# Second layer of a two-layer transformer on one core: the first attention on its latent, the last batch's gating on two engines, weights loaded earlier

## The reference

```python
# third block: 8 heads of 64, latent of 64
q = (x @ Wq.T).reshape(b, t, 8, 64)
kv_latent = x @ Wkv_down.T
k = (kv_latent @ Wk_up.T).reshape(b, t, 8, 64)
v = (kv_latent @ Wv_up.T).reshape(b, t, 8, 64)
scores = einsum('bqhd,bkhd->bhqk', q, k) * 64 ** -0.5
out = einsum('bhqk,bkhd->bqhd', softmax(scores), v).reshape(b, t, 512) @ Wo.T
# fourth block
wv = topk_mask(x @ Ws, 2) * sigmoid(x @ Ws)              # b t h e
v = einsum('bthe,btek->bhtk', wv, einsum('btd,edk->btek', x, Wv))
attn = softmax attention of (x @ Wq) and (x @ Wk) over v
out = einsum('bthe,bthk,ekd->btd', topk_mask(x @ Wd, 2), attn, Wo)
```

## Time and profile before

| | |
|---|---|
| three timed runs | 3288.48, 3310.31, 3311.98 us, median 3310.31 |
| the profiled execution | 3291.7 us, its span 3289.6 us |
| busy over the span | PE 2514.8 us (76%), DVE 2017.9 (61%), POOL 1914.4 (58%), ACT 1706.0 (52%) |
| second layer | from 1784.5 us to the end |
| mean granted clock of TensorE | 0.845 of full speed (2.4 GHz; 0.5 is the lower level, 1.2 GHz) |

### The profile page before, as it was taken

The page is one execution under the profiler, slowest core; times in us unless marked ns, Lnnn a source line. Parts: engine busy times, 40 slices in busy tenths (PEclk is TensorE's granted clock), DMA queues, the critical chain, the costliest instruction groups (busy, mean ns, idle before and its releaser), DMA issues. The chain is left out here.

```text
span 3289.6 us, 31482 instructions
## 1 busy us (share of the span) xinstructions
PE 2514.8 (76%) x10185; PEld 1158.7 (35%) x10185; DVE 2017.9 (61%) x3044; ACT 1706.0 (52%) x2409; POOL 1914.4 (58%) x1911
## 2 busy tenths in 40 slices
PE   4567676766766676752994889899999999999984
PEld 2222222322322232221552344444444444444432
DVE  4798878687868787731332366565647464656541
ACT  1677776776776777850221345444444444444440
POOL 0555566666665675864775106565748383746495
PEclk7678787877777777775997899999999999999996
DMA  2000000000101000011997100000000000000000
GB/s 90 14 0 7 9 14 15 13 14 15 14 15 14 15 7 7 15 21 38 268 267 197 20 1 1 1 14 7 14 7 1 20 1 20 1 7 1 7 1 13
DMA packets 94883, 99.04 MB, mean 30 GB/s; under 512 B 19552, under 2 KB 91488, under 8 KB 94688
## 3 DMA queue, kind: packets, MB, share of 16 engines
q1 hardware_dynamic: 69984, 73.53, 7.9%
q0 software_dynamic: 24704, 23.22, 3.9%
HBM read 74.24 MB, written 26.80 MB: 31 GB/s over the span
## 5 line engine op out<-in xcount | busy, mean ns | idle before, releaser
L848 POOL TENSOR_TENSOR TT<-TT,SS 128x512 f32<-128x512 f32 x512 | 652.1, 1308 | 401.8 <-ACT SS L779 401.5
L1467 ACT ACTIVATE PR<-S,NM 128x512 f32<-128x512 f32 x512 | 347.5, 683 | 589.3 <-DVE NM L1588 589.3
L1588 DVE TENSOR_REDUCE NM<-S 128x2 f32<-128x1024 f32 x256 | 313.1, 1223 | 254.0 <-PE S L1382 252.4
L371 PE MATMUL OB<-TT,VAL 128*17 128x512 f32 x1024 | 349.4, 786 | 86.9 <-ACT TT L787 86.9
L612 DVE TENSOR_SCALAR TT<-SC 128x1024 f32<-128x1024 f32 x256 | 311.4, 1216 | 121.4 <-POOL TT L848 60.7
L1382 PE MATMUL S<-KT,QT 64*128 64x512 f32 x1024 | 328.4, 661 | 0.0
L614 DVE SCALAR_TENSOR_TENSOR SS<-SC,TT 128x1024 f32<-128x1024 f32 x256 | 313.5, 1225 | 20.2 <-issue 1.3
L853 POOL DMA_INDIRECT slot_tokens<-TID,IDX x256 | 258.9, 1011 | 111.7 <-issue 84.7
L1411 PE MATMUL OT<-PT,VN 128*64 128x512 f32 x1024 | 283.5, 633 | 3.1 <-ACT PT L1473 2.3
L1393 PE MATMUL TP<-ident,PR 128*128 128x128 f32 x2048 | 274.6, 277 | 3.9 <-DVE PT L1593 3.0
L1393 PEld LDWEIGHTS TP<-ident,PR 128*128 128x128 f32 x2048 | 226.6, 141 | 143.3 <-issue 117.5
(11 more groups left out here) (227 smaller groups left out, 4281.7 us busy)
## 6 DMA issues: line engine op xcount, KB each, us to landing
WG<-w_gu SPq DMA_DIRECT2D x64, 384.0 KB
WD<-w_dn SPq DMA_DIRECT2D x64, 128.0 KB
stream<-rows SPq DMA_DIRECT2D x1, 4224.0 KB, 16.5
XL<-x SPq DMA_DIRECT2D x8, 512.0 KB, 4.2
X<-x SPq DMA_DIRECT2D x8, 512.0 KB, 3.9
rows<-XL SPq DMA_DIRECT2D x8, 512.0 KB, 8.9
slot_tokens<-TID,IDX POOLq DMA_INDIRECT x256
stream<-X SPq DMA_DIRECT2D x8, 512.0 KB, 3.6
```

What stands on the lines that cost most here:

```text
L371: ins = pe.matmul(OB[r:r + DH0 + 1, :], values_of[:, mt, h, :], TT[:, h % RING, mt, :], start=(mt == 0), stop=(mt == NT - 1))
L848: ins = pool.tensor_tensor(tt[:, mt, :], tt[:, mt, :], ss[:, mt, :], ALU.add)
L1467: act.activation(PR[s % 2][h2][:], S[s % 2][:, h2, :], ACT.Exp, bias=NM[:, s % 2, h2:h2 + 1], accum_out=SM[:, pair % 2, j, h2:h2 + 1]).the ...
L1588: dve.tensor_reduce(NM[:, s % 2, :], S[s % 2][:], AX, ALU.max, negate=True).then_inc(sems["peak"], 1)
```

## The change

**First attention in the latent space.** With q = x Wq and k = c Wk (c the latent), q k' = (x Wq Wk') c'. So Wq and Wk of a head are multiplied once into a combined weight `q1a` (width 64 a head, as before), the keys of all heads are the latent, and no `keys1` is left. In the same way the values are the latent (`values1` is now one item of four transposes of it), and Wv goes into the output weight `o1a`. `down1` is loaded twice side by side, so that the latent lies on both halves of the partitions. The combining is new: `absorb` ahead of run 0 (16 transposes into banks of S, 16 small products, five ACT copies) and two items `absorb_out` in run 0. Three `queries1` of batch 0 and its `values1` move from `FIRST` into run 0.

**Start.** SP loads both streams of batch 0, DVE adds them and does the normalisation itself. The weights Wq, Wkv_down, Wk_up, Wv_up are loaded in `stage_two`, after expert 3's.

**Last batch's gating.** POOL gates the odd heads into a buffer of its own (`gate_last`, h = 2 * pair + 1), DVE the even ones into another, `join` adds the two. The last batch's `turn_out2` and `product_out2` use the seven other PSUM banks instead of `BK`.

```diff
@@ stage_two, SP @@
                 sp.dma_start(WD[u][P - FC:P, 1, :], w_dn[e][P:F, :]).then_inc(sems[f"weights_in{u}"], 16)
+                if e == UN - 1:
+                    for dst, src in early:
+                        sp.dma_start(dst, src).then_inc(sems["weights_now"], 16)
@@ tables @@
 PREP_1 = table(
-    (0, 4, 1, "turn_norm", 0), (0, 5, 1, "turn_norm", 1), (0, 5, 2, "latent", 0),
-    (0, 6, 1, "queries1", 0), (0, 6, 2, "keys1", 0), (0, 7, 2, "queries1", 1), (0, 8, 1, "keys1", 1),
-    (0, 9, 1, "queries1", 2), (0, 9, 2, "keys1", 2), (0, 10, 1, "queries1", 3), (0, 10, 2, "keys1", 3),
-    (0, 11, 2, "values1", 0), (0, 12, 1, "values1", 1), (0, 13, 1, "values1", 2), (0, 14, 1, "values1", 3))
+    (0, 4, 1, "turn_norm", 0), (0, 5, 1, "turn_norm", 1), (0, 6, 1, "latent", 0), (0, 8, 1, "queries1", 0),
+    (0, 9, 1, "values1", 0), (0, 10, 1, "queries1", 1), (0, 12, 1, "queries1", 2), (0, 13, 1, "queries1", 3))
+PREP_FIRST = table((0, 0, 1, "queries1", 1), (0, 1, 1, "values1", 0), (0, 2, 1, "queries1", 2), (0, 3, 1, "queries1", 3),
+                   (0, 8, 2, "absorb_out", 0), (0, 11, 1, "absorb_out", 1))
-OUT_2_TAIL = table((0, 4, 3, "turn_out2", 0), ...
+OUT_2_TAIL = table((0, 4, 3, "join", 0), (0, 4, 3, "turn_out2", 0), ...
-    FIRST = table((0, 0, 3, "merge", 0), (0, 0, 3, "stats", 0), ..., (0, 0, 3, "latent", 0),
-                  *[(0, 0, 3, part, i) for i in range(C1) for part in ("queries1", "keys1")],
-                  *[(0, 0, 3, "values1", j) for j in range(NT)])
+    FIRST = table((0, 0, 3, "absorb", 0), (0, 0, 3, "stats_first", 0), ...,
+                  (0, 0, 3, "latent", 0), (0, 0, 3, "queries1", 0))
@@ stage_three, SP @@
-            for b in range(2):
-                sp.dma_start(X[b][:], x_b[b]).then_inc(sems[f"x_in{b}"], 16)
-            for dst, src in loads_now:
-                sp.dma_start(dst, src).then_inc(sems["weights_now"], 16)
-            for b in range(2, XN_RING):
+            sp.dma_start(X[0][:], x_b[0]).then_inc(sems["x_in0"], 16)
+            sp.dma_start(XN[:], x2_b[0]).then_inc(sems["x_in0"], 16)
+            for b in range(1, XN_RING):
@@ TensorE @@
+            def values1(v, i, b):
+                bank = item(v, "free_d")
+                need(v, "latent", b, 0)
+                for j in range(NT):
+                    ins = pe.transpose(bank[:, j * R1:(j + 1) * R1], KT[set_for(1, b)][0:R1, 0, j * P:(j + 1) * P],
+                                       ident[0:R1, 0:R1])
+            def absorb(v, i, b):
+                pe.wait_ge(sems["weights_now"], 16 * NOW)
+                ...
+                pe.wait_ge(sems["wide_in"], 3)
+                for c in range(DC):
+                    for pair in range(PAIRS1):
+                        for h2 in range(2):
+                            lo, at = DH1 * h2, (PAIRS1 * c + pair) * R1
+                            ins = pe.matmul(TP[h2][:, at:at + R1], q1t[lo:lo + DH1, pair, c * P:(c + 1) * P],
+                                            kvt[lo:lo + DH1, 0, pair, :], start=True, stop=True)
+            def absorb_out(v, i, b):
+                bank = item(v, "free_a")
+                for a in range(2):
+                    for h2 in range(2):
+                        lo, pair = DH1 * h2, 2 * i + a
+                        ins = pe.matmul(bank[lo:lo + R1, a * D:(a + 1) * D], kvt[lo:lo + DH1, 1, pair, :],
+                                        o1[lo:lo + DH1, pair, :], start=True, stop=True)
@@ scores, attend @@
-                                    KT[r % 2][lo:lo + DH1, pair, :], start=True, stop=True)
+                                    KT[r % 2][lo:lo + DH1, 0 if kind == 1 else pair, :], start=True, stop=True)
-                    h, lo = 2 * pair + h2, DH1 * h2
+                    h, lo = 2 * pair + h2 if kind == 2 else 0, DH1 * h2
@@ DVE @@
+            def stats_first(v, i, b):
+                dve.wait_ge(sems["x_in0"], 32)
+                dve.tensor_tensor(flat, flat, XN[:].rearrange("p j d -> p (j d)"), ALU.add)
+                dve.drain()
+                measure(X[0])
+                dve.wait_ge(sems["rstd1"], 1)
+                for j in range(NT):
+                    ins = dve.tensor_scalar(XN[:, j, :], X[0][:, j, :], mv[:, j, 0:1], rstd[:, j:j + 1],
+                                            ALU.subtract, ALU.mult)
+            def gate(v, pair, b):
+                if b < B - 1:
+                    return
+                h = 2 * pair
+                dve.drain()
+                for j in range(NT):
+                    ins = dve.tensor_tensor((gt if pair else gl)[:, j], ..., ALU.mult)
+                if pair:
+                    dve.drain()
+                    ins = dve.tensor_tensor(GL_DVE, GL_DVE, GT_DVE, ALU.add)
+            def join(v, i, b):
+                dve.wait_ge(sems["gadd"], H1 * B)
+                dve.drain()
+                dve.tensor_tensor(GL_POOL, GL_POOL, GL_DVE, ALU.add).then_inc(sems["joined"], 1)
```

More of the change, by code:

```diff
@@ L1108, in timetable @@
             put(r, OUT_2, b - 1)
+    put(0, PREP_FIRST, 0)
     for b in range(1, XN_RING):
@@ L1186, in stage_three @@
     READER = dict(
-        turn_norm="dd", latent="a", queries1="aaaa", keys1="dada", values1="adad", product_out1="dddd", gates="d",
+        turn_norm="dd", latent="a", queries1="aaaa", values1="d", absorb_out="aa", product_out1="dddd", gates="d",
         experts="aaaa", queries2="aaaa", keys2="aaaa", turn_out2="ddd", product_out2="dddd",
     )
-    FIRST = table((0, 0, 3, "merge", 0), (0, 0, 3, "stats", 0), *[(0, 0, 3, "turn_norm", c) for c in range(DC)], (0, 0, 3, "latent", 0),
-                  *[(0, 0, 3, part, i) for i in range(C1) for part in ("queries1", "keys1")],
-                  *[(0, 0, 3, "values1", j) for j in range(NT)])
+    FIRST = table((0, 0, 3, "absorb", 0), (0, 0, 3, "stats_first", 0), *[(0, 0, 3, "turn_norm", c) for c in range(DC)],
+                  (0, 0, 3, "latent", 0), (0, 0, 3, "queries1", 0))
     def reader(part, i):
@@ L1331, in turn_out2 @@
             def turn_out2(v, c, b):
-                bank = item(v, "free_d")
-                if c == 0:
+                last = b == B - 1
+                bank = free_bank(c) if last else item(v, "free_d")
+                if last and c == 0:
+                    pe.wait_ge(sems["joined"], 1)
+                elif c == 0:
                     pe.wait_ge(sems["gadd"], v.next("gadd", H1))
@@ L1336, in turn_out2 @@
                 for j in range(NT):
-                    ins = pe.transpose(bank[:, j * P:(j + 1) * P], GO[:, j, lo:lo + P], ident[:])
+                    ins = pe.transpose(bank[:, j * P:(j + 1) * P], (GL_POOL if last else GO)[:, j, lo:lo + P], ident[:])
                 ins.then_inc(sems["item_d"], 1)
             def product_out2(v, j, b):
-                bank = item(v, "free_d")
+                bank = free_bank(3 + j) if b == B - 1 else item(v, "free_d")
+                if b == B - 1 and v.all_due("free_d"):
+                    pe.wait_ge(sems["free_d"], v.value + 3)
                 for c in range(3):
@@ L1378, in scores @@
                     need(v, f"queries{kind}", b, pair)
-                    need(v, f"keys{kind}", b, pair)
+                    need(v, *(("latent", b, 0) if kind == 1 else ("keys2", b, pair)))
+                if (r, s) == (0, 0):
+                    pe.wait_ge(sems["wide_in"], 5)
                 for h2 in range(2):
@@ L1406, in attend @@
                         pe.wait_ge(sems["vh"], v.next("vh", 2))
[L1407 to L1408 removed]
+                if kind == 1 and pair == 0 and m == 0:
+                    need(v, "values1", b, 0)
                 for h2 in range(2):
[L1410 removed]
+                    h, lo = 2 * pair + h2 if kind == 2 else 0, DH1 * h2
                     ins = pe.matmul(OT[lo:lo + DH1, :], VN[r % 2][:, m, h * DH1:(h + 1) * DH1], PT[pair % 2][h2][:, m, :],
@@ L1544, in product_out2 @@
                 dve.wait_ge(sems["item_d"], v.next("item_d"))
-                dve.tensor_tensor(x[:, j, :], x[:, j, :], BK[:, 0:D], ALU.add).then_inc(sems["free_d"], 1)
+                bank = free_bank(3 + j) if b == B - 1 else BK
+                dve.tensor_tensor(x[:, j, :], x[:, j, :], bank[:, 0:D], ALU.add).then_inc(sems["free_d"], 1)
                 if j == NT - 1:
@@ L1673, in mix_values, with gate_last @@
                     ins.then_inc(sems["vh"], 1)
+            def gate_last(v, pair, b):
+                pool.wait_ge(sems["head"], v.next("head"))
+                pool.drain()
+                gl = GL_POOL.rearrange("p j (e d) -> p j e d", e=SE)
+                gt = GT[:].rearrange("p j (e d) -> p j e d", e=SE)
+                h = 2 * pair + 1
+                for j in range(NT):
+                    ins = pool.tensor_tensor((gt if pair else gl)[:, j], AH[pair % 2][:, j, 1, :].unsqueeze(1).to_broadcast([P, SE, DH1]),
+                                             MO[b % 2][:, j, h, :].unsqueeze(2).to_broadcast([P, SE, DH1]), ALU.mult)
+                if pair:
+                    pool.drain()
```

(5 more changed lines are left out.)

124 lines of the change are left out of this document (89 added, 35 removed).

## The result

| | before | after |
|---|---|---|
| timed, median (lowest to highest) | 3309.01 us (3288.48 to 3311.98) | 3197.28 us (3192.03 to 3206.46) |
| profiled execution, span | 3291.7, 3289.6 us | 3206.46, 3204.7 us |
| second layer begins | 1784.5 us | 1800.9 us |
| second layer, to the end | 1505.1 us | 1403.8 us |

The account below looks back on a forecast made before the run. TensorE's own time bounds the second-attention runs, a serial chain the start, GpSimd the tail. -47 + 2 - 38 + 0.5 - 30 = -112.5 us from 3291.7 gives 3179, plus 10 = 3189 us, range 3162 to 3222.

Parts of the forecast that it names:

- Part 1: Six second-attention runs: dropping keys1 and values1 products saves 7.8 us a run, -47 us, bounds -52 to -30.
- Part 2: run 0: added queries1, values1 and absorb_out against dropped products, +2 us, bounds -2 to +8.
- Part 3: Second layer's start: no merging DMA, DVE adds and normalises x; first reduction by 1810, -38 us, bounds -30 to -42.
- Next late is TensorE's weight work: Second layer's start: weight work, through at 1791.5 to 1798, about meets normalised x at 1796.3 and is next to be late.
- Part 4: Tail: gating shared by GpSimd and DVE, no buffer wait, seven banks; -30 us, bounds -18 to -37.
- The split: Last batch's gating: GpSimd spared four heads of 5.94 us, less 6 us of lock and 1.4 of join, 16 us.
- if the heads are there. They are: Tail: the third pair's heads are ready at 3221, the fourth's at 3227, so GpSimd need not wait.
- (a): Tail: DVE and GpSimd lock each other, DVE's gates delay reductions; gain 12 instead of 30 us, 3207; chance 0.13.
- The offset (+10): Whole program: 10 us added to 3179, placing the forecast in the middle of the timed runs' two levels.
- (b): Second-attention runs: dropped products come back as waits, half of 47 us lost, 3212; chance 0.12.
- (c): Six lightened runs: clock falls to the lower level, each losing 59 us, not gaining 7.8; three give 3390; chance 0.03.
- (d): Second layer's start: TensorE's weight work not done when x is, 8 us late, 3197; counted within the forecast's 0.70.

Follow-up runs that it names:

- run 0: Not an experiment: the second layer's first run, a run being one attention of one batch in 16 steps; 70.8 us before, 68.5 after.
- t12: The kernel before, unchanged, timed and profiled a second time: 3310.65 us, ratio 1.0002.
- run 2: Not an experiment: a second-attention run of one batch in the second layer, one of six lightened; 79.3 us before, 71.1 after.
- t5: The changed kernel with eight extra half products put back in each of the seven runs ahead of a first attention: 3277.62 us.
- t6: The changed kernel with the second and third turning of the previous batch's output one slot earlier, ahead of DVE's reciprocal: 3171.55 us.
- t11: The kernel before with only the two moved timetable rows of t6: 3288.52 us, ratio 0.9935.
- t4: The changed kernel with the five weight loads issued at the second layer's start, behind batch 0's two loads, not during the experts: 3199.85 us.
- t3: The changed kernel with GpSimd instead of DVE doing the four normalisations of batch 0: 3194.49 us.
- run 15: Not an experiment: the second layer's last run, an attention of the last batch; first reduction to the end 155.5 us before, 134.5 after.
- t1: The changed kernel with GpSimd gating all eight heads of the last batch in its own buffer, no DVE gating and no join: 3209.59 us.
- t7: The changed kernel with DVE's gating of the last batch's second pair moved behind the last step's reductions: 3192.65 us.
- t8: The changed kernel with the last batch's heads dealt anew, GpSimd gating 1, 2, 3 and 5, DVE 0, 4, 6 and 7: 3190.13 us.
- t2: The changed kernel with the last batch's turnings and products in the one shared bank again: 3198.68 us.
- run 4: Not an experiment: a second-attention run of one batch in the second layer, one of six lightened; 81.4 us before, 74.8 after.
- t9: The changed kernel with the timetable of t6, GpSimd gating only heads 1 and 2 of the last batch, DVE the other six: 3162.27 us.
- t10: t9 with the turnings, gates and experts' products of the second attention's preparation one step or slot later: 3158.21 us.

## Why the prediction was right, and where it was off

The time came out 8 us above the forecast and inside the range; the layer's gain was forecast as 112.5 and measured as 101.3 and 110.0 against the two profiles of before. Part of that is luck. Worked from the first profile and measured against it, the sum is 11 us too large, 9 of them in the tail; the medians lie 112 us apart all the same, because other executions of the kernel before are longer than that profile, in places of which the sum knew nothing (t12: 7.3 us in the start and run 0).

**Part 1 (-47): right.** 44.0 us against the first profile, 46.0 against the second (491.3 for the six runs). In run 2, which has no stall, the products gave 8.2 us where the sum had 7.8. That TensorE's time is the price of every product is shown by t5 and t6. What the step did not see is that the stall in step 3, then 7.7 or 9.2 us, would be 9.4 each time: 1.7 us in each run that had 7.7. The stall was in the trace of before, and reading step lengths inside a run would have shown it; that it would be the longer one each time, the trace did not say.

**Part 2 (+2): wrong in sign, and just outside its bounds (-2 to +8).** Run 0 got 2.3 us shorter (5.3 against t12). The two `absorb_out` took 1.08 us each, near the lower bound of 0.9 and not the 1.8 taken, which is 1.4 us of the 4.3. And a wait of run 0 before, behind a copy of DVE, is gone with the keys:

```profile
1895.53 1.98 PE L1278 MATMUL BK<-XT,q1s 128*128 128x512 f32 x4 [2.05 <-DVE KT L1515]
```

After, the longest wait of TensorE in that stretch of run 0 is 0.98 us, ahead of the second `absorb_out`.

**Part 3 (-38): right as a sum, one step wrong.** The first reduction came after 28.1 us, 35.5 earlier; but the same start took 25.5 to 29.1 us in nine executions and 63.6, 67.2 (t11) and 67.95 before, so one pair of profiles tells this part only to some 4 us. The add of x began at 6.2 us and not 5.1, and DVE's four normalisations took 2.44 us where 1.4 was taken; in t4 the same four took 1.38. In the changed kernel and the eight others with its start GpSimd began to issue three DMAs as these began, and they took 2.44 us each time; in t4 the first was issued 1.1 us later. One case against nine, and t4 differs in more than this: that the DMAs are the reason is only argued. "Next late is TensorE's weight work" was wrong: it was done 6 us before x. t4 put it there, and that cost 2.3 us. t3, beside executions with the clock at its higher level as early, shows that 2.9 us more in this chain come through as 2.1 to 2.7. The early loads were put at +0.5; they cost nothing measurable.

**Part 4 (-30): right in direction, the term of the split mis-sized.** Banks: 3.9 against 4.4. A product came every 3.15 us and not every 2.9. Own buffer: 8.6 against 8.6. The split: 8.6 us, where the sum had 16 (four heads of 5.94 less 6 us of lock and 1.4 of join), so the last turning came 17.2 us earlier and not 25. The step that failed is "if the heads are there. They are". The sum had GpSimd done at 3239.3, 105.2 us after the first reduction of run 15; it was done at 112.7. The lock was sized well in total: GpSimd began 1.1 us later than taken, its first two heads took 1.2 us longer and its last two 3.8 (15.7 against 2 x 5.94), 6.1 us where 6 were taken. The other 7.5 us are the wait of 7.53 us for the third pair's heads. They were taken to be there at 3221, which is 86.9 us, and came at 96.1. Rival (a) had named why: "DVE's gates at steps 9 and 13 delay the reductions". t1, t7 and t8, without the gate of step 13, have them at 88.2 to 88.6. How much of the 7.5 us the end gets back depends on where that gating goes: 3.3 in t7, where the wait moved to the fourth pair, and 5.1 in t8, where the heads were dealt anew.

**The offset (+10).** The forecast put the profiled execution between two levels of the timed runs. That profile lay 17.3 us under the median of 3309.0. If t12's layer is the usual one, which is not shown, 8.7 of them are in the second layer and the rest in the first part. The median itself less 112.5 would have given 3196.5. Most of the 8 us that the forecast is off is this choice, and it hides the 11 us by which the sum was too large for the profile it was worked from.

**The rivals.** (a) was about half true: the tail gave 21, between 30 and 12. (b) is excluded by run 2, where the whole 8.2 us left, and by t5. (c), the clock, is there on a small scale: 0.98 in the lightened runs, by a wait and not by lightness; t6 has less waiting and the same work, and 1.00. (d) is excluded, since the weight work was done 5.9 us ahead of x; t4 shows what it would have cost.

## What to carry to other kernels

Before counting products, list the waits of the bounding engine inside one repeated unit of work; a copy queued behind a long operation on its engine (here 3.34 us) costs its wait each time, and two rows of a table moved gave 26 us, more than all the work on the tail (21). GpSimd's gating and DVE's with two SBUF inputs take turns here: deal such work by the price on each engine almost as if they were one, and above all keep it away from copies on which the last steps wait (t7 and t8 gave 3.3 and 5.1 us that way, taking two more heads from GpSimd 0.8). One profile of a kernel whose executions differ is one sample: compare parts of it that repeat exactly.

## What was not expected of the hardware

- The runs 0 to 14 of the second layer repeat within 0.3 us from execution to execution in the changed kernel and t1, t2, t4 (run 4: 74.7, 74.8, 74.8, 74.8 us; in t3 one run differed, 76.4 for 74.8). The start of the layer does not: the same code took 25.5 to 29.1 us, and the moment at which the granted clock rose lay between 20.6 and 30.7 us. The first part, the same code too but for the five loads, lasts from 1784.5 to 1809.8 us.
- The same product behind the same 2.66 us wait took 1.54 or 2.80 us in one execution (t5). Such a spell at the lower clock follows some waits and not others.
- Behind 15.8 us of an idle TensorE (t9, and t10 too) the level rose during the turnings and products of the tail, 0.84 of full speed in t9; behind 14.1 and 16.8 us (after, t8) it stayed at 0.50 to the end, 16.4 us of work. Why was not tried.
